# First batch, handover to the experts and final sums in another order, in a transformer layer kernel

## The chip, the cores and the metric

One core of a Trainium2 chip runs the whole program in one launch. The metric is the time of the slowest core on the device, in microseconds (us); there is one core here. Each kernel is timed over several runs, and one more execution is profiled.

## The reference

```python
x = x + attention(layernorm(x))     # x: 8 batches x 512 tokens x 256 channels
                                    # 16 heads of 16, rotary embedding, causal
x = x + moe(layernorm(x))           # 8 experts, top 2 of 8, capacity 153 per batch and expert
# moe: logits = h @ router_w + b ; p = softmax(top2(logits))
#      position of a token in its expert's buffer by a cumulative count over the batch
#      o = (silu((t @ w_c_fc + b1) * (t @ w_gate + b2))) @ w_c_proj + b3   (hidden 1024)
#      result = sum over the two experts of p * o[expert, position]
```

Layer norm has no weights. All is computed in float32. A product of float32 values is made of three TensorE products of high and low parts (`hi*hi + lo*hi + hi*lo`, `product3`, L79), so each operand is first split into a high part (rounded to fp32r) and a low part.

## The kernel before, in words

**Attention.** Batches run in a software pipeline of slots `(b, g, u)`: batch b, group g of four heads, slot u of eight. Each engine (SP for DMA issues, PE, ACT, DVE, POOL) runs its own hand-written list of what it does in a slot. The first batch has a prologue (`b = -1`): `load_x`, layer norm statistics on DVE (L729, L734), the inverse root on POOL (`rsqrt`, L947 to L955, three Newton steps, 14 instructions that each wait for the one before), `normalise` on DVE (L739), two sets of four transposes on PE ("X", L485), `xnT` split into high on ACT (L640) and low on DVE (L811), the q, k, v projections ("Q", "V"), the rotary embedding on DVE and POOL (L855, L856, L861, L973), and a high and low part `hilo` of the rotated q and k. SP stores `hilo[:, n]` to DRAM (`store_hilo`, L342; n = 0 is q and n = 1 is k of the first 128 channels, 512 KB each) and loads it back rearranged as `qst` and `kst` (`load_stack`, L355, 256 KB each, four per group of heads). PE's scores of a group (L450) wait for its four loads. Before the first projections, ACT copies the three weights to their high parts (L685) and DVE makes the low parts (L892) in the same queues.

**Handover.** The last batch's output row `x1` (L826), its second layer norm, router, slot numbers and scatter of token rows to `slot_tokens` are not done in the attention slots any more. `LATE_SLOTS` hangs them between the steps of the first expert: key -2 and -1 ahead of expert 0, key k behind step k (a step is one of 8 chunks of the hidden layer for one of three row blocks, so keys 0 to 7 are block 0, 8 to 15 block 1). In each slot stands an attention slot such as `(8, 3, 4)`, the last root on POOL, or `(9, 0, 1)`, the transposes of `hn`. The block 2 rows of expert 0 need the last scatter.

**Experts.** In each step PE makes the fc and gate products (`up`, L79), ACT adds the bias (L1458), DVE multiplies (`gated`, L1570), ACT applies silu (L1426), DVE casts to the high part `ah` (L1498), POOL makes the low part `al` (L1610). silu(k) waits for al(k-2). PE may be two steps ahead of `gated`. Behind step 2 PE projects the block before (`project`), and DVE adds the bias and writes `o_sb` (`tiles_out`, L1557), which SP stores to `slot_outputs`. POOL also splits the next expert's weights, one slice a step (L1644, L1649). The first expert's own weights are split by `split_first_hi` (L1098) and `split_first_lo` (L1103).

**Final sums.** In expert 7 POOL has no weights to split and gathers each token's two output rows from `slot_outputs` by indirect DMA (`gather`, L1675, four of 128 rows per batch and kind): the low ones (kind 0, expert numbers below) and the high ones (kind 1), each as soon as its stores have landed; the high ones of batches 5, 6 and 7 need the last tiles. `combine(b, k)` (L1542) on DVE adds four tiles of `share * gathered` to `y`, which starts as the residual `x1` that ACT's queue loads (`load_y`, L1438). ACT's queue also stores the results (`store_y`, L1443). `y` has four buffers for eight batches: a load for batch 4 to 7 waits for the store of batch b - 4. Where each stands is given by `LOAD_Y_AT` and `STORE_Y_AT` (block, step), `COMBINE_AT` (expert, block, tile) and `COMBINE_LAST`.

## Time and profile before

| What | us |
|---|---|
| Median of 3 runs (1255.8 to 1259.39) | 1258.95 |
| The profiled execution, its own time | 1255.67 |
| its span, first to last instruction | 1253.9 |
| busy: PE 1173.1 (94%), DVE 728.7, POOL 680.8, ACT 483.2 | |
| mean granted TensorE clock | 0.979 |
| issue of one stack load (L355) on SP's queue | 0.59 to 0.70 |
| a step of 384 columns on PE in the experts | 2.1 |
| a projection of three tiles on PE | 8.5 |
| POOL per step: split high 0.40, `al` 1.00, split low 0.74 | 2.15 |
| router: the two selections of one batch in the handover (L745 to L765), 563.50 to 567.3 | 3.8 |
| `split_first_lo` of one weight on DVE (L1103) | 2.28 |
| four tiles of a combine on DVE / one | 1.67 / 0.48 |
| `normalise`, four tiles, with POOL idle | 1.4 |
| wait of PE for `pv_sb` ahead of the first expert | 0.8 |
| end of the statistics of the last `x1` on DVE | 538.4 |

The span's busy shares are means over stages; what a wait costs is read in its stage. In the rows further down, times are in us from the span's start, durations in us, and in brackets stands how long the engine was idle before the group and what released it.

### The profile page before, as it was taken

How to read it: one execution, taken by the hardware profiler on the slowest of the kernel's cores; microseconds unless marked ns; L12 is line 12 of the kernel's file. 1: busy time of each engine (PE TensorE's matmuls, PEld its weight loads, DVE VectorE, ACT ScalarE, POOL GpSimd, SP SyncE). 2: the span in 40 equal slices, each digit the busy share in tenths (PEclk: the TensorE clock that was granted, in tenths of full speed). 3: DMA queues.
4: the chain of work that ended last, by engine and by line, in shares of the span. 5: the costliest groups of instructions: out<-in, count | busy, mean ns of one | idle time of the engine just before them, and what ended most of it. 6: DMA issues, size and time to landing. Idle time of an engine off the chain costs nothing.

```text
span 1253.9 us, 24021 instructions
## 1 busy us (share of the span) xinstructions
PE 1173.1 (94%) x8264; PEld 997.7 (80%) x8264; DVE 728.7 (58%) x1525; ACT 483.2 (39%) x988; POOL 680.8 (54%) x974
## 2 busy tenths in 40 slices
PE   4699999999999999878999999999999999999992
PEld 3466667676666666578999999999998999999992
DVE  5677788888888876656533333343333333434665
ACT  2146454545554545533332233233333222332320
POOL 4234342626363540677666556576665655667735
PEclk9699999999999999989999999999999999999996
DMA  5866845555555555333122122121211211304436
GB/s 138 222 238 193 243 120 151 139 149 151 140 147 144 143 141 148 118 135 107 60 69 64 64 73 98 41 96 59 69 59 62 73 64 65 113 26 132 147 122 209
DMA packets 83134, 148.24 MB, mean 118 GB/s; under 512 B 9647, under 2 KB 60728, under 8 KB 78910
## 3 DMA queue, kind: packets, MB, share of 16 engines
q1 hardware_dynamic: 65344, 111.37, 31.1%
q0 software_dynamic: 7936, 26.60, 6.3%
q10 hardware_dynamic: 9728, 8.67, 2.2%
q8 instruction: 69, 1.13, 0.4%
q14 instruction: 57, 0.47, 0.1%
HBM read 93.05 MB, written 53.61 MB: 117 GB/s over the span
## 4 chain that ended last, share of the span: by engine, by line
PE 49%; POOL 18%; issue 17%; DVE 9%; DMA 4%; ACT 2%; POOLq 0%; SPq 0%; DVEq 0%; ACTq 0%
PE ps L79 26%; POOL al L1610 8%; PE ps L450 5%; PE ps L479 4%; PE ps L468 3%; DVE mx L838 3%; PE ps L485 2%; PE ps L523 2%; POOL wp_lo L1649 2%; POOL wg_lo L1649 2%; PE ps L462 1%; DVE rope_s L855 1%; PE ps L441 1%; POOL wf L1649 1%; POOL wp_hi L1644 1%
## 5 line engine op out<-in xcount | busy, mean ns | idle before, releaser
L1610 POOL TENSOR_TENSOR al<-hid,ah 128x384 fp32r<-128x384 f32 (+1 forms) x168 | 179.3, 1067 | 209.0 <-DVE ah L1498 209.0
L1458 ACT ACTIVATE fc<-ps,b_fc 128x384 f32<-128x384 f32 (+1 forms) x192 | 115.4, 601 | 437.5 <-PE ps L79 436.4
L1570 DVE SCALAR_TENSOR_TENSOR gated<-ps,b_gate,fc 128x384 f32<-128x384 f32 (+1 forms) x192 | 123.2, 642 | 222.4 <-PE ps L79 201.8
L838 DVE TENSOR_REDUCE mx<-ps 128x2 f32<-128x256 f32 (+3 forms) x256 | 206.5, 819 | 34.2 <-PE ps L450 32.6
L450 PE MATMUL ps<-kst,qst 65*128 65x256 f32 (+2 forms) x512 | 149.1, 374 | 10.8 <-DMA kst<-qk_parts 10.8
L619 ACT ACTIVATE probs<-ps 128x512 f32<-128x512 f32 (+1 forms) x256 | 122.8, 542 | 54.4 <-PE ps L468 53.1
L1557 DVE TENSOR_TENSOR o_sb<-ps,b_proj 128x256 f32<-128x256 f32 x80 | 33.9, 424 | 153.9 <-PE ps L79 153.8
L1426 ACT ACTIVATE hid<-gated 128x384 f32<-128x384 f32 (+1 forms) x192 | 102.8, 536 | 25.8 <-POOL al L1610 14.4
L611 ACT ACTIVATE probs<-ps 128x256 f32<-128x256 f32 (+1 forms) x128 | 62.6, 490 | 128.2 <-PE ps L462 127.2
L79 PE MATMUL ps<-xh,wg_hi 128*128 128x384 f32 (+1 forms) x384 | 103.0, 349 | 3.7 <-DVE gated L1570 3.7
L79 PE MATMUL ps<-xl,wg_hi 128*128 128x384 f32 (+1 forms) x384 | 102.5, 348 | 0.0
L79 PE MATMUL ps<-xh,wg_lo 128*128 128x384 f32 (+1 forms) x384 | 102.3, 348 | 0.0
L1498 DVE CAST ah<-hid 128x384 fp32r<-128x384 f32 (+1 forms) x192 | 90.8, 473 | 9.5 <-ACT hid L1426 9.5
L479 PE MATMUL ps<-probs,v_sb 128*17 128x512 f32 (+3 forms) x1024 | 93.8, 438 | 0.0
L79 PE MATMUL ps<-xh,wf 128*128 128x384 f32 (+1 forms) x384 | 89.3, 354 | 1.6 <-DVE xl L1409 0.9
L450 PEld LDWEIGHTS ps<-kst,qst 65*128 65x128 f32 x512 | 80.2, 198 | 11.1 <-DMA kst<-qk_parts 11.0
L79 PE MATMUL ps<-wp_hi,ah 128*128 128x256 f32 (+1 forms) x632 | 87.6, 281 | 1.4 <-DVE posm L778 0.9
L79 PE MATMUL ps<-wp_lo,ah 128*128 128x256 f32 (+1 forms) x632 | 87.5, 281 | 0.0
L79 PE MATMUL ps<-wp_hi,al 128*128 128x256 f32 (+1 forms) x632 | 87.3, 280 | 0.0
L973 POOL TENSOR_TENSOR rope_c<-qk_b,rope_table 128x512 f32<-128x512 f32 x32 | 43.7, 1365 | 75.4 <-ACT qk_b L647 75.3
L79 PEld LDWEIGHTS ps<-wp_hi,ah 128*128 128x128 f32 (+1 forms) x632 | 80.8, 183 | 2.6 <-issue 1.2
L79 PEld LDWEIGHTS ps<-wp_lo,ah 128*128 128x128 f32 (+1 forms) x632 | 79.8, 184 | 0.0
(194 smaller groups left out, 2461.9 us busy)
## 6 DMA issues: line engine op xcount, KB each, us to landing
qk_parts<-hilo SPq DMA_DIRECT2D x32, 512.0 KB, 3.7
qst<-qk_parts SPq DMA_DIRECT2D x64, 256.0 KB, 5.0
kst<-qk_parts SPq DMA_DIRECT2D x64, 256.0 KB, 5.6
slot_tokens<-zeros POOLq DMA_DIRECT2D x12, 816.0 KB, 5.9
rows<-slot_tokens SPq DMA_DIRECT2D x24, 384.0 KB, 3.6
slot_outputs<-o_sb SPq DMA_DIRECT2D x72, 128.0 KB, 1.7
raw<-in_wf SPq DMA_DIRECT2D x8, 1024.0 KB, 6.8
raw<-in_wg SPq DMA_DIRECT2D x8, 1024.0 KB, 6.8
```

Source lines behind the costliest of these rows:

```text
L79: last = nc.tensor.matmul(out, w, x, start=(i == 0), stop=(i == len(terms) - 1))
L450: last = mm(bank, qst[0:MROW, g, h, bass.ts(i, P)], kst[0:MROW, g, h, 0:width], start=False, stop=True, skip_group_check=True)
L479: last = mm(pvb[32 * h:32 * h + DH + 1, P * j:T], v_sb[:, bt % 2, j, GH * g + h, :], probs[:, j % 2, h, P * j:T], start=(j == 0), stop=(j ...
L611: A(probs[:, j % 2, 2 * pr:2 * pr + 2, P * j:T], in_pairs(banks2(u)[0])[:, :, P * j - q0:T - q0], ACT.Exp, scale=float(DH) ** -0.5).then_i ...
L619: A(probs[:, j % 2, 2 * pr + hh, P * j:T], ps[:, banks2(u)[hh], P * j - q0:T - q0], ACT.Exp, scale=float(DH) ** -0.5).then_inc(exp_done, 1)
L838: V.reduce_max(mx[:, g % 2, 2 * pr:2 * pr + 2, i], both[:, :, 0:P * (i + 1)], AXX)\
L1426: A(hid[:, hc % 2, 0:width], gated[:, hc % 2, 0:width], ACT.Silu).then_inc(hid_done, 1)
L1458: A(fc[:, hc % 2, 0:width], ps[:, FC + hc % 2, 0:width], ACT.Identity, bias=b_fc[:, e, hc:hc + 1]).then_inc(fc_out, 1)
L1498: V.tensor_copy(ah[:, (8 * n + hc) % RING, 0:width], hid[:, hc % 2, 0:width]).then_inc(ah_done, 1)
L1570: V.scalar_tensor_tensor(gated[:, hc % 2, 0:width], ps[:, GATE + hc % 2, 0:width], b_gate[:, e, hc:hc + 1], fc[:, hc % 2, 0:width], ALU.ad ...
L1610: G.tensor_tensor(al[:, at, 0:width], hid[:, hc % 2, 0:width], ah[:, at, 0:width].bitcast(F32), ALU.subtract).then_inc(al_done, 1)
L1649: ins = G.tensor_tensor(w_lo[1 - par][n][:, cols], src, w_hi[1 - par][n][:, cols].bitcast(F32), ALU.subtract)
```

## The change

- Batch 0's inverse root moves from POOL to DVE (`root`, 11 chained instructions), and so does the root of the last batch's second layer norm; the other roots stay on POOL. The memsets of `base` and `v_sb` go to the front of DVE's list. On ACT and DVE the evictions of the first transposes come ahead of the weights' high and low parts. SP loads the rotary table ahead of `wvT`.
- The first two stores of `hilo` are cut in halves of 64 channels, each with a semaphore; the q loads of the first stack wait only for q's half, the k loads for k's.
- `LATE_SLOTS`: the root in key 1 of DVE, `hn` in key 2 in place of 3; transposes, router and scatters one key earlier; `split_first_lo(2)` in step 4 in place of 2 and with a wait for itself ahead of the count.
- `y` gets eight buffers (four of them over gathered rows that are already summed), residual loads start at step 0 of expert 7, all low sums are made before the last steps, batches 5 to 7 are combined tile by tile as each gather lands (`FINE = 5`), and their results go out in halves.

```diff
@@ -340,6 +341,21 @@
         sp.dma_start(dst.rearrange("h p t -> p h t"), hilo[:, n].bitcast(F32)).then_inc(st_hilo[n // 2], 16)
+    def store_first(n, part):
+        wait(sp, hilo_done, n + 1)
+        side = slice(GH * DH * part, GH * DH * (part + 1))
+        dst = rt["qk"][0, n, :, side, :].rearrange("h p t -> p h t")
+        sp.dma_start(dst, hilo[side, n].bitcast(F32)).then_inc(st_hilo[0] if part else st_first[n], 16)
+    def load_first_stack(n):
+        sp.wait_ge(st_first[n], 16)
+        for i in range(2):
+            q = rt["qk"][0, 0, :, 0:GH * DH, :].rearrange("c (d h) t -> d c (h t)", h=GH)
+            k = rt["qk"][0, 1, i, 0:GH * DH, :].rearrange("(d c h) t -> d c (h t)", h=GH, c=1)\
+                .to_broadcast([DH, 2, GH * T])
+            rows = (qst, kst)[n][2 * DH * i:2 * DH * (i + 1), 0].rearrange("r h t -> r (h t)").bitcast(F32)
+            sp.dma_start(rows, (q, k)[n]).then_inc(ld_stack[0], 16)
@@ -391,14 +407,19 @@
     for i, (w_sb, name) in enumerate(((raw_q, "wqT"), (raw_k, "wkT"), (raw_v, "wvT"))):
+        if i == 2:
+            sp.dma_start(rope_table, d["consts"][:, 0:2 * T]).then_inc(ld_w, 16)
...
-    sp.dma_start(rope_table, d["consts"][:, 0:2 * T]).then_inc(ld_w, 16)
...
-    for n in range(4):
+    store_first(0, 0)
+    store_first(1, 0)
+    store_first(0, 1)
+    load_first_stack(0)
+    load_first_stack(1)
+    store_first(1, 1)
+    for n in range(2, 4):
...
-        if n == 1:
-            load_stack(0, 0)
@@ -680,11 +701,11 @@
     A(lgT[:, 0:1], wr[:, 0, E:E + 1], ACT.Exp)
+    body_slot(-1, 0, 7)
+    body_slot(-1, 1, 0)
...
-    body_slot(-1, 0, 7)
-    body_slot(-1, 1, 0)
@@ -738,6 +759,19 @@
                                   ALU.subtract, ALU.mult)
+        ins.then_inc(done, 1)
+    def root(chain, mv, rs, done):
+        v, y, a = rs[:, 0, :], rs[:, 1, :], rs[:, 2, :]
+        chain(V.tensor_scalar(v, mv[:, :, 1], EPS, None, ALU.add))
+        chain(V.tensor_scalar(y.bitcast(I32), v.bitcast(I32), -0.5, RSQRT_MAGIC, ALU.mult, ALU.add))
+        for it in range(3):
+            chain(V.tensor_tensor(a, y, y, ALU.mult))
+            chain(V.scalar_tensor_tensor(a, a, -0.5, v, ALU.mult, ALU.mult))
+            ins = V.scalar_tensor_tensor(y, a, 1.5, y, ALU.add, ALU.mult)
+            if it < 2:
+                chain(ins)
@@ -863,6 +897,10 @@
             layer_stats(chain, x1, stats2, mv2, mv2_done)
+        if (g, u) == (3, 4) and isinstance(b, int) and b == BATCH:
+            dve.wait_ge(mv2_done, BATCH)
+            dve.wait_ge(rs2_done, BATCH - 1)
+            root(chain, mv2, rs2, rs2_done)
@@ -883,7 +921,11 @@
     V.memset(wr[:], 0.0).then_inc(wr_set, 1)
+    chain(V.memset(base[:], float(E * EROWS)))
+    chain(V.memset(v_sb[:], 1.0))
...
+    dve.wait_ge(mv1_done, 1)
+    root(chain, mv1, rs1, rs1_done)
@@ -897,19 +939,17 @@
-    split_lo(0)
-    split_lo(1)
-    body_slot(chain, -1, 0, 7)
-    body_slot(chain, -1, 1, 0)
-    split_lo(2)
...
-    chain(V.memset(base[:], float(E * EROWS)))
-    chain(V.memset(v_sb[:], 1.0))
+    body_slot(chain, -1, 0, 7)
+    body_slot(chain, -1, 1, 0)
+    split_lo(0)
+    split_lo(1)
+    split_lo(2)
@@ -1026,7 +1066,7 @@
     G.memset(zeros[:], 0.0).then_inc(z_ready, 1)
-    for g, u in ((0, 1), (1, 2), (1, 5), (1, 7), (2, 2)):
+    for g, u in ((1, 2), (1, 5), (1, 7), (2, 2)):
@@ -1099,8 +1140,10 @@
 eng.wait_ge(w_half, j + 1)
+ops.tensor_tensor(w0[1][j], raw[:, j % 2, :], w0[0][j].bitcast(F32), ALU.subtract).then_inc(w_lo_done[j], 1)
+eng.wait_ge(w_lo_done[j], 1)
...
-ops.tensor_tensor(w0[1][j], raw[:, j % 2, :], w0[0][j].bitcast(F32), ALU.subtract).then_inc(w_ready, 1)
+eng.sem_inc(w_ready, 1)
@@ -1111,12 +1154,12 @@
 "pe": {-2: ((8, 2, 3),), -1: ((8, 2, 5), (8, 2, 6)), 0: ((8, 3, 1), (8, 3, 2)),
-   5: ((9, 0, 1), (9, 0, 2)), 6: ((9, 0, 4),), 7: ((9, 0, 5),), 9: ((9, 1, 5),)},
-"act": {-2: ((8, 2, 2),), -1: ((8, 2, 6), (8, 2, 7)), 5: ((9, 0, 2), (9, 0, 3)), 6: ((9, 0, 5),), 8: ((9, 1, 4),)},
-"dve": {-2: ((8, 2, 4),), 0: ((8, 3, 2), (8, 3, 3)), 1: ((8, 2, 6),), 3: ((8, 3, 7),),
-    7: ((9, 0, 6), (9, 1, 1), (9, 1, 2)), 9: ((9, 1, 6), (9, 2, 1)), 10: ((9, 2, 6),)},
-"pool": {-1: ((8, 2, 3), (8, 2, 4), (8, 2, 6)), 0: ((8, 3, 4),),
-     9: ((9, 2, 1), (9, 2, 3), (9, 2, 4), (9, 2, 6))},
+   4: ((9, 0, 1), (9, 0, 2)), 5: ((9, 0, 4),), 6: ((9, 0, 5),), 8: ((9, 1, 5),)},
+"act": {-2: ((8, 2, 2),), -1: ((8, 2, 6), (8, 2, 7)), 4: ((9, 0, 2), (9, 0, 3)), 5: ((9, 0, 5),), 7: ((9, 1, 4),)},
+"dve": {-2: ((8, 2, 4),), 0: ((8, 3, 2), (8, 3, 3)), 1: ((8, 3, 4),), 2: ((8, 3, 7),), 3: ((8, 2, 6),),
+    6: ((9, 0, 6), (9, 1, 1), (9, 1, 2)), 8: ((9, 1, 6), (9, 2, 1)), 10: ((9, 2, 6),)},
+"pool": {-1: ((8, 2, 3), (8, 2, 4), (8, 2, 6)),
+     8: ((9, 2, 1), (9, 2, 3), (9, 2, 4), (9, 2, 6))},
@@ -1182,29 +1225,37 @@
 got_late = [half for w_ in (w_hi, w_lo) for half in in_batches(w_[0][2][:].bitcast(F32))]
-y = [half for i in range(2) for half in in_batches(raw[:, i, :])]
+spent = Region(nc, rt["early"])
+spent.skip(4 * 2 * 2 * HID)
+y_rows = [raw[:, 0, :], raw[:, 1, :], spent.take("y_spent0", [P, 2 * HID])]
+spent.skip(2 * 4 * 2 * HID)
+y_rows.append(spent.take("y_spent1", [P, 2 * HID]))
+y = [half for tile in y_rows for half in in_batches(tile)]
+FINE = 5
...
-got_low, got_high = ([sem(f"got_{kind}{b}") for b in range(BATCH)] for kind in ("low", "high"))
-ld_y = [sem(f"ld_y{i}") for i in range(len(y))]
-st_y = [sem(f"st_y{i}") for i in range(len(y))]
-summed, low_sum = sem("summed"), sem("low_sum")
+got_low, got_high = ([sem(f"got_{kind}{b}") for b in range(n)] for kind, n in (("low", BATCH), ("high", FINE)))
+ld_y = [sem(f"ld_y{i}") for i in range(BATCH // 2)]
+st_y = sem("st_y")
+summed, low_sum, half_sum = sem("summed"), sem("low_sum"), sem("half_sum")
+got_row = [[sem(f"got_row{b}_{i}") for i in range(TT)] for b in range(FINE, BATCH)]
...
-LOAD_Y_AT = ((0, 3), (0, 4), (0, 5), (0, 6))
-STORE_Y_AT = ((2, 6), (2, 7))
+LOAD_Y_AT = ((0, 0), (0, 1), (0, 2), (0, 3), (0, 4), (0, 5), (0, 7), (1, 1))
+STORE_Y_AT = ((2, 4), (2, 5))
+COMBINE_IN = {(0, 5): (2, 0), (0, 7): (3, 0), (1, 5): (7, 0), (2, 5): (2, 1)}
...
-    (LAST, 0, 1): ((2, 0),), (LAST, 0, 2): ((3, 0),),
+    (LAST, 0, 0): ((4, 0),), (LAST, 0, 1): ((5, 0),), (LAST, 0, 2): ((6, 0),),
...
-    (LAST, 2, 0): ((2, 1),), (LAST, 2, 1): ((3, 1),), (LAST, 2, 2): ((4, 0),), (LAST, 2, 3): ((5, 0),),
+    (LAST, 2, 0): ((3, 1),), (LAST, 2, 1): ((4, 1),),
...
-COMBINE_LAST = ((4, 1), (6, 0), (5, 1), (7, 0), (6, 1), (7, 1))
+COMBINE_LAST = ((5, 1), (6, 1), (7, 1))
@@ -1388,9 +1438,9 @@
-    late_slots("pe", 0, -2)
...
+    late_slots("pe", 0, -2)
@@ -1433,14 +1483,19 @@
             act.wait_ge(rt["st_x1"], 16 * BATCH)
-        if b >= len(y):
-            act.wait_ge(st_y[b % len(y)], 16)
-        act.dma_start(y[b % len(y)], batch_rows(rt["x1"], b)).then_inc(ld_y[b % len(y)], 16)
+        if b >= BATCH // 2:
+            act.wait_ge(low_sum, b - BATCH // 2 + 1)
+        act.dma_start(y[b], batch_rows(rt["x1"], b)).then_inc(ld_y[b % (BATCH // 2)], 16)
...
-        act.wait_ge(summed, b + 1)
-        act.dma_start(batch_rows(d["out"], b), y[b % len(y)]).then_inc(st_y[b % len(y)], 16)
+        if b < FINE:
+            act.wait_ge(summed, b + 1)
+            act.dma_start(batch_rows(d["out"], b), y[b]).then_inc(st_y, 16)
+            return
+        for i in range(2):
+            act.wait_ge(half_sum, 2 * (b - FINE) + i + 1)
+            act.dma_start(batch_rows(d["out"], b)[:, 2 * i:2 * i + 2], y[b][:, 2 * i:2 * i + 2]).then_inc(st_y, 16)
@@ -1471,13 +1526,7 @@
-    load_y(4)
-    load_y(5)
-    store_y(2)
-    load_y(6)
-    store_y(3)
-    load_y(7)
-    for b in range(len(y), BATCH):
+    for b in range(2, BATCH):
@@ -1530,18 +1579,25 @@
+        fine = k == 1 and b >= FINE
...
-            dve.wait_ge(ld_y[b % len(y)], 16 * (b // len(y) + 1))
+            dve.wait_ge(ld_y[b % (BATCH // 2)], 16 * (b // (BATCH // 2) + 1))
...
-            dve.wait_ge(got_high[b], 16 * TT)
+            if not fine:
+                dve.wait_ge(got_high[b], 16 * TT)
...
-            ins = V.scalar_tensor_tensor(y[b % len(y)][:, t, :], src[:, t, :], share[:, k, col:col + 1],
-                                         y[b % len(y)][:, t, :], ALU.mult, ALU.add)
-        ins.then_inc((low_sum, summed)[k], 1)
+            if fine:
+                dve.wait_ge(got_row[b - FINE][t], 16)
+            ins = V.scalar_tensor_tensor(y[b][:, t, :], src[:, t, :], share[:, k, col:col + 1],
+                                         y[b][:, t, :], ALU.mult, ALU.add)
+            if fine and t % 2 == 1:
+                ins.then_inc(half_sum, 1)
+        if not fine:
+            ins.then_inc((low_sum, summed)[k], 1)
@@ -1575,11 +1631,13 @@
                     sort_entries(hc)
-                if isinstance(e, int) and (e, n, hc) == (0, 0, 2):
+                if isinstance(e, int) and (e, n, hc) == (0, 0, 4):
...
+                if isinstance(e, int) and e == LAST and (n, hc) in COMBINE_IN:
+                    combine(*COMBINE_IN[n, hc])
@@ -1675,7 +1733,8 @@
                 in_offset=bass.IndirectOffsetOnAxis(ap=row_of[:, k, col:col + 1], axis=0),
-                bounds_check=there_now - 1, oob_is_err=False).then_inc((got_low, got_high)[k][b], 16)
+                bounds_check=there_now - 1, oob_is_err=False)\
+                .then_inc(got_row[b - FINE][t] if k == 1 and b >= FINE else (got_low, got_high)[k][b], 16)
```

## Rows read from the trace of the kernel before

**Rows 1.** Windows: length, busy PE, PEld, DVE, ACT, POOL, PEclk, DMA, GB/s.
```profile
39.00:60.00 21.00, 17.80 (x68) 12.26 (x68) 14.70 (x30) 2.83 (x5) 5.34 (x17) 0.58 0.96 261
545.00:560.00 15.00, 7.32 (x48) 6.64 (x46) 6.40 (x11) 5.35 (x11) 13.69 (x30) 0.77 0.19 69
610.00:1150.00 540.00, 537.37 (x3494) 522.63 (x3493) 203.73 (x417) 173.39 (x344) 338.25 (x458) 1.00 0.21 71
```

**Rows 2.** Timeline, first batch: start, us, engine, line, operation, idle before it.
```profile
10.88 1.38 DVE L739 TENSOR_SCALAR xn<-x_in,mv,rs 128x256 f32<-128x256 f32 x4 [4.01 <-POOL rs L955]
...
12.77 0.69 DVE L892 TENSOR_TENSOR wq_lo<-raw_q,wq_hi 128x512 fp32r<-128x512 f32 x1 [0.51 <-ACT wq_hi L685]
...
14.86 1.06 ACT L640 ACTIVATE xnT_hi<-ps 128x512 fp32r<-128x512 f32 x2
15.47 1.29 DVE L811 TENSOR_TENSOR xnT_lo<-ps,xnT_hi 128x512 fp32r<-128x512 f32 x2 [1.04 <-ACT xnT_hi L640]
...
16.91 1.19 PE L79 MATMUL ps<-xnT_hi,wq_hi 128*128 128x512 f32 x2 [2.57 <-DVE xnT_lo L811]
...
18.59 1.87 DVE L912 MEMSET v_sb<- 128x2176 f32 x1 [0.54 <-DVE base L911]
...
39.13 0.79 PE L450 MATMUL ps<-kst,qst 65*128 65x256 f32 x2 [10.75 <-DMA kst<-qk_parts]
```

**Rows 3.** Timeline of PE, expert 0: transposes of hn and last rows.
```profile
554.65 1.94 PE L485 MATMUL ps<-consts_sb,hn 128*128 128x128 f32 x8 [7.68 <-DVE hn L739]
...
589.35 0.98 PE L1332 MATMUL ps<-consts_sb,rows 128*128 128x128 f32 x8 [1.34 <-DMA rows<-slot_tokens]
```

**Rows 4.** Timeline of POOL, last root, first al after it, last scatters.
```profile
544.93 0.22 POOL L947 TENSOR_SCALAR rs<-mv 128x4 f32<-128x4 f32 x1
...
549.11 0.99 POOL L1610 TENSOR_TENSOR al<-hid,ah 128x384 fp32r<-128x384 f32 x1
...
573.71 1.13 POOL L1005 DMA_INDIRECT slot_tokens<-hn,put_at  x1 [1.44 <-DVE put_at L790]
```

**Rows 5.** Timeline of ACT, expert 0.
```profile
550.19 0.52 ACT L1426 ACTIVATE hid<-gated 128x384 f32<-128x384 f32 x1 [8.19 <-POOL al L1610]
```

**Rows 6.** Timeline of PE, expert 7, after that combine.
```profile
1156.29 0.62 PE L79 MATMUL ps<-xh,wg_hi 128*128 128x384 f32 x2 [2.27 <-DVE gated L1570]
```

**Rows 7.** Timeline of DVE, expert 7: combine of batch 1.
```profile
1153.70 1.67 DVE L1542 SCALAR_TENSOR_TENSOR raw<-wf_hi,share,raw 128x256 f32<-128x256 f32 x4 [7.98 <-DMA raw<-x_rows]
```

**Rows 8.** Timeline of POOL, gathers in expert 7 and after it.
```profile
1154.00 1.06 POOL L1675 DMA_INDIRECT wf_lo<-slot_outputs,row_of  x1 [0.31 <-issue]
...
1227.18 0.99 POOL L1675 DMA_INDIRECT wp_hi<-slot_outputs,row_of  x1 [8.84 <-issue]
...
1231.08 3.17 POOL L1675 DMA_INDIRECT wp_hi<-slot_outputs,row_of  x1 [0.30 <-issue]
...
1241.30 2.86 POOL L1675 DMA_INDIRECT wp_lo<-slot_outputs,row_of  x1 [0.30 <-issue]
...
1245.77 0.99 POOL L1675 DMA_INDIRECT wp_lo<-slot_outputs,row_of  x1 [0.30 <-issue]
```

**Rows 9.** Timeline of DVE, the last combine.
```profile
1248.64 1.67 DVE L1542 SCALAR_TENSOR_TENSOR raw<-wp_lo,share,raw 128x256 f32<-128x256 f32 x4 [5.36 <-DMA wp_lo<-slot_outputs,row_of]
```

**Rows 10.** Timeline of DVE, small steps of one chain (four of them).
```profile
490.78 0.16 DVE L770 TENSOR_SCALAR dlt<-ex 128x4 f32<-128x4 f32 x1
...
491.39 0.17 DVE L773 TENSOR_TENSOR prob_all<-ex,dlt 128x4 f32<-128x4 f32 x1
```

**Rows 11.** Chain of waits, first 45 us: start, us, what.
```profile
28.46 2.75 DMA qk_parts<-hilo
...
33.19 5.89 DMA kst<-qk_parts
```

**Rows 12.** DMA issues, whole span: KB each, median us to landing.
```profile
slot_outputs<-o_sb SPq DMA_DIRECT2D x72, 128.0 KB, 1.7
...
out_rows<-raw ACTq DMA_DIRECT2D x8, 512.0 KB, 3.3
```

11 lines of the change are left out of this document (6 added, 5 removed).

## Prediction

> **What bounds the kernel now.** Durations without a group stand in the table of the profile above. I read the windows first. From 610 to 1150 us TensorE is busy 537.4 of 540 us at the full clock [rows 1], and the change edits nothing there. Time can only come from the three places that it edits: the first batch, the handover from attention to experts, and the end. For those I read the chain of waits and then each engine's timeline.
>
> *First batch.* TensorE's first scores start at 39.13, after 10.75 us of waiting for the key stack [rows 2]. Before that the chain is serial: statistics, the root on POOL (VectorE idle for 4.01), xn, transposes, the two splits of xnT, projections, rotation, the store, the load of the stack.
>
> *Handover.* TensorE stands 7.68 us before it transposes the last batch's hn and 1.34 before the last token rows [rows 3]. The first is a knot of queues: POOL does its root of 14 steps from 544.93, ahead of the first `al`, at 549.11 [rows 4]; ScalarE's next silu waits 8.19 for that `al` [rows 5]; VectorE's cast waits for the silu, and hn stands behind the cast.
>
> *End.* Expert 7 loses 2.27 on TensorE [rows 6], because VectorE waited 7.98 for a residual load that ScalarE's queue issued only after the projection [rows 7]. After TensorE is done, 12 gathers leave POOL from 1227.18 on, 1.3 apart (0.99 and a gap of 0.30), except two that take 3.17 and 2.86. The last is issued at 1245.77 [rows 8], its combine starts at 1248.64 [rows 9], and one 512 KB store follows.
>
> **The change, part by part.**
>
> *Root of batch 0 on VectorE.* POOL's 14 steps go and VectorE gets 11. Four chained steps of VectorE on small tiles lie 0.20 apart: 490.78 to 491.39 is three pitches [rows 10]. So 11 x 0.21 = 2.3 in place of 4.0, a gain of 1.7. xn starts at 9.2 rather than 10.88 and ends at 10.6. The memset of v_sb (1.87) [rows 2] and the tiny one of base move in front; x takes longer than that to land, so they cost nothing. Had x landed at once, they would cost 1.9.
>
> *Transposes before weight splits.* The 8 transposes take 1.94 on a cold clock, as the same eight do later [rows 3], so they end at 12.6. The last xnT_hi (1.06 for two) ends at 13.1 and its xnT_lo (1.29 for two) at 13.8. wq is now copied behind xnT_hi and split behind xnT_lo: 0.69 for the split [rows 2], ending at 14.5. VectorE's five bf16 casts move ahead of this, while it waits for the transposes. Q0 starts at 14.7 instead of 16.91: 2.2 gained, the root included. The table of rope passes raw_v in SP's queue; wv is needed last of the three, so I cost this at nothing. All that follows up to the second `hilo` keeps its order, so it moves by 2.2.
>
> *Half stores.* Now: the store after the second `hilo` takes 2.75, then four loads of some 0.65 each to issue, of which the last goes out at 33.19 and lands 5.89 after that [rows 11]. From 28.46 that is 4.73 to the last issue. New: two half stores (0.55 each to issue), two q loads (0.65 each) while the k half store lands, one k load: the last issue is 3 x 0.65 + 2 x 0.55 = 3.1 after `hilo`, and 3.3 with the wait for the k half, 1.4 gained. A half store is 256 KB; between 1.7 for 128 KB and 3.3 for 512 KB [rows 12] it takes about 2.2, so it is down before the k loads. But the loads fill the DMA engines (0.96 busy from 39 to 60) [rows 1], and the remaining halves and later stores now share them, so I take 1.2. Bounds: 0 if the engines' throughput sets the landing, 1.7 if the half store lands at once. A rule speaks against this part: the Trainium skill ("DMA: Bandwidth & Descriptors", the section "Anatomy of one DMA") gives a DMA some 2 us however small, plus its bytes at 436 GB/s, and the section "Bandwidth" advises large ones. By an estimate from that page a half store still takes 2.6 and this part brings 0.8, not 1.2; the 1.7 for 128 KB in the rows is under its fixed part, so I stay with the rows.
>
> First batch: 2.2 + 1.2 = 3.4, between 2.2 and 3.9. The later stacks land before their turn, so I let all of it through.
>
> *Handover* (on the time axis of before, without the shift of the first batch). The root goes to VectorE at step 1, hn to step 2, split_first_lo(2) from 2 to 4, and all router pieces one step earlier. POOL's first `al` moves up by 3.9. Statistics end at 538.4, the root takes 2.3 behind one gated product: 542.2. Then the next product and cast, and hn of 1.4: 544.6. TensorE reaches the H pieces at 544.6: the 7.68 is gone. What is late next? ScalarE's copies of hT stand behind silu(3), which waits for the second `al`, at 548.4: hT is out at 550.2, and TensorE, done with its next step at 547.8, waits 2.4. From there POOL's pace is 2.15 per step, about TensorE's own 2.1. VectorE adds the split (2.28) and the router's two selections (about 4.0), which hold `onehot` to 559; scatters start at 565.1 instead of 573.71 [rows 4], and the last rows are transposed at 581 rather than 589.35 [rows 3]. Gain 8.0. Bounds: 3.9, the root alone; 10.2, if the route does not fall behind the split. The sem_inc behind the split costs 0.1 on VectorE. Moving turn 0 before the A piece fills a wait of 0.8 for pv_sb and costs nothing.
>
> *Low sums earlier.* ScalarE now issues its residual loads from step 0 on, so the 2.27 goes. The price: the first load waits for the last weight split of POOL, and ScalarE's first step is some 2.5 late; TensorE runs two steps ahead on banks, so I charge 0.3, which the projection's slack gives back. VectorE gets low combines (1.67 each) at steps 5, 7 and 13 and waits at two of them for gathers, up to 2.6 behind; TensorE's slack is 2.1 per step, so I charge nothing. If that cover were gone, each late combine would cost up to 1.7.
>
> *End.* Before, at the two long gathers VectorE ran 8 and 12 combine rows in a stretch while 512 KB residual loads and stores filled the DMA engines. Both causes leave: low combines and loads are done by then. So 3.17 + 2.86 - 2 x 0.99 = 4.05 comes out of the chain. The last combine is one row of 0.48 and not four (1.67): 1.2. The last store is 256 KB: 3.3 - 2.2 = 1.1. With the 2.27: 8.6. Bounds: 4.6 if the long gathers stay, 9.0 if the last landing (2.8) is also quicker, with less in flight.
>
> Sum: 3.4 + 8.0 + 8.6 = 20.0. The profiled execution took 1255.67 for a span of 1253.9; less 20.0 that is 1235.7. It lies 3.3 below the median of the three runs, which would give 1239.0. I say 1237.
>
> **Rivals.**
>
> *The gathers stay long.* If the stall is POOL's own ring that fills when transfers queue, 12 gathers 1.3 apart can still fill it. The gain is then 16, so 1241. For it: both long ones came after several in flight. Against: the other 62 gathers took 1.32 at most, many of them with three in flight too.
>
> *Each row's combine holds the next gather.* A gather beside a combine took 1.06 [rows 8], against 0.99, so the hold is small by this row. If each of the 11 combine rows that now fall between gathers held one up by its whole 0.48, the end would get 5.3 back and the gain would be 14.7: 1242. That is how the Trainium skill ("SBUF — State Buffer", the section "SBUF: two separate sides") describes VectorE with two SBUF inputs, or in a two-port mode, against GpSimd: the other blocks for the whole instruction.
>
> *The handover gives the root only.* If `al` and hid pace it and the router falls behind split_first_lo, 3.9 comes and not 8: gain 16, 1241.
>
> *Slower.* From 545 to 560 the granted clock was 0.77 in the mean, and from 39 to 60, with small waits, 0.58 (near 1.2 GHz) [rows 1]. If the new wait of 2.4 at the L piece leaves it at 1.2 GHz, TensorE's work from there to the last rows, 10 steps of 2.1 and a projection of 8.5, takes twice its 29.5: 1237 + 29.5 = 1266. It decides from 22 us of doubled work on, 44 us at the low clock. For it: one wait of 7.68 was enough to pull the mean to 0.77. Against it: from 39 to 60 the clock did come back, with waits beside it.
>
> *It does nothing:* each path is hidden behind another, 1259. Against it: TensorE or the last gathers stand alone on the chain in every one of the three.
>
> **How the numbers follow.** Forecast (all three parts) 0.63; long gathers 0.13; combine holds gathers 0.10; root only 0.10; low clock 0.02; nothing 0.02. The bounds of the parts sum to gains of 10.7 and 23.1 together; from the median the first is 1248, from the profiled execution the second is 1232. Range 1231 to 1247. A measurement of this kernel tells 0.3% (3.8 us) from no change; all cases but the last two are faster by more: faster 0.95, same 0.03, slower 0.02.
>
> **What would show it.** xn at 9.2, Q0 at 14.7, the first scores near 35.7; hn before 545 + the shift of the first batch, with no wait of 7.68 at its transposes but one of 2 to 3 at L; the last token rows near 578; no wait of VectorE for residual loads in expert 7; the 12 last gathers 1.3 apart with none over 1.5, and 2.8 from the last one to its one combine row. It is wrong if the key stack lands after 37, if a new wait over 4 stands in the handover, if gathers beside single combine rows take 1.4, or if the clock stays at half after 545.

## The result, and the profile after

The changed kernel took 1244.0 us in the median (1242.8 to 1245.3, 4 runs) against 1258.5 for the kernel before (1255.8 to 1259.4, 4 runs): ratio 0.9888, 95% interval 0.9868 to 0.9909. That is 14.5 us less where 20 were forecast; 1244 lies inside the range. The profiled execution has a span of 1240.8 against 1253.9. The sections below show that some 3.4 of these microseconds come from something the forecast did not contain, and that two of its three sums were too large.

**First batch**, timeline of VectorE and TensorE after the change, for [rows 2]:

```profile
7.12 0.17 DVE L767 TENSOR_SCALAR rs<-mv 128x4 f32<-128x4 f32 x1
...
9.10 0.16 DVE L772 SCALAR_TENSOR_TENSOR rs<-rs 128x4 f32<-128x4 f32 x1
9.30 1.38 DVE L760 TENSOR_SCALAR xn<-x_in,mv,rs 128x256 f32<-128x256 f32 x4
...
14.03 0.68 DVE L934 TENSOR_TENSOR wq_lo<-raw_q,wq_hi 128x512 fp32r<-128x512 f32 x1
...
14.77 1.22 PE L79 MATMUL ps<-xnT_hi,wq_hi 128*128 128x512 f32 x2 [2.01 <-DVE wq_lo L934]
...
35.64 0.80 PE L471 MATMUL ps<-kst,qst 65*128 65x256 f32 x2 [9.44 <-DMA kst<-qk_parts]
```

The root's 11 steps start at 7.12 and end at 9.26; xn starts at 9.30, Q0 at 14.77, the scores at 35.64. The forecast said 9.2, 14.7 and 35.7. The half stores themselves were slower than it said (2.2); the DMA issues of this profile give their size and the median from issue to landing:

```profile
qk_parts<-hilo SPq DMA_DIRECT2D x4, 256.0 KB, 3.3
```

**Handover**, waits of TensorE from 545 to 600 us (us in total, times, longest), then its timeline and POOL's first `al`, for [rows 3, 4]:

```profile
PE ps L79 <- DVE xl L1459: 3.0, 2, 2.7
PE ps L567 <- DVE onehot_bf L798: 2.3, 1, 2.3
PE ps L555 <- ACT hT L679: 1.8, 1, 1.8
...
544.47 1.00 POOL L1668 TENSOR_TENSOR al<-hid,ah 128x384 fp32r<-128x384 f32 x1
...
582.01 0.96 PE L1382 MATMUL ps<-consts_sb,rows 128*128 128x128 f32 x8
...
587.87 0.68 PE L79 MATMUL ps<-xh,wf_hi 128*128 128x456 f32 x2 [2.75 <-DVE xl L1459]
```

The wait of 7.68 for hn is gone, one of 1.80 stands at the L piece, and the last rows are transposed at 582.01 instead of 589.35, without a wait. But there is a new one, 2.75 for `xl`, ahead of block 2. That block starts at 587.87; before it started at 592.96. So 7.3 us of lead at the rows are 5.1 at the block behind them. (The forecast had the rows near 578 with the first batch's lead; the third batch's xn stands at 99.5 in both profiles, so that lead does not show here. In a second profile of the changed kernel it does, and the rows are at 579.8.)

**Expert loop.** Nothing in it was changed, and yet TensorE gained 1.7 us there twice. Timeline of VectorE at the two returns of the loop over experts, in the kernel before, and at the first of them after:

```profile
796.12 0.62 DVE L1570 SCALAR_TENSOR_TENSOR gated<-ps,b_gate,fc 128x384 f32<-128x384 f32 x1 [4.66 <-issue]
...
966.26 0.62 DVE L1570 SCALAR_TENSOR_TENSOR gated<-ps,b_gate,fc 128x384 f32<-128x384 f32 x1 [4.67 <-issue]
```
```profile
788.19 0.62 DVE L1626 SCALAR_TENSOR_TENSOR gated<-ps,b_gate,fc 128x384 f32<-128x384 f32 x1 [1.77 <-ACT fc L1513]
```

Before, VectorE stood 4.7 us at each return (the jump back to the first instruction of the loop) with nothing that the profile shows to wait for ("issue"). After, it waits 1.77 for ScalarE, as a step normally does.

**End.** Waits of TensorE from 600 us on, the 12 last gathers (first and last), the last combine row and the stores, for [rows 6 to 9, 12]:

```profile
PE ps L79 <- DVE xl L1459: 2.2, 2, 1.3
...
1219.24 1.00 POOL L1733 DMA_INDIRECT wp_hi<-slot_outputs,row_of  x1 [9.64 <-issue]
1220.54 1.00 POOL L1733 DMA_INDIRECT wp_hi<-slot_outputs,row_of  x1 [0.30 <-issue]
...
1233.57 1.00 POOL L1733 DMA_INDIRECT wp_lo<-slot_outputs,row_of  x1 [0.30 <-issue]
...
1236.50 0.48 DVE L1595 SCALAR_TENSOR_TENSOR y_spent<-wp_lo,share,y_spent 128x256 f32<-128x256 f32 x1 [0.33 <-DMA wp_lo<-slot_outputs,row_of]
...
out_rows<-y_spent ACTq DMA_DIRECT2D x6, 256.0 KB, 2.8
slot_outputs<-o_sb SPq DMA_DIRECT2D x6, 128.0 KB, 1.7
```

None of these 12 gathers took over 1.0; they need 14.3 us from the first issue to the last, against 18.6. VectorE waits for no residual load. In the place of TensorE's 2.27 [rows 6] there are 1.28 and 0.88 for `xl`. The last combine row starts 2.93 behind the last gather's issue (forecast 2.8), but 3.82 us pass between its end and the end of the span, no less than before (3.59).

### How the profiles are compared

Profiles of the same code differ in one stretch by more than the changes that are to be seen. So each profile is cut at the same instructions: the first scores, `xn` of the third batch, POOL's first `al` of expert 0, block 2 of expert 0, one expert's first tile to the same tile an expert later (`o_sb` of experts 2 to 3 and 4 to 5, the loop's returns), the first tile of expert 6, the first of the last 12 gathers, the last gather, the end. Durations in us:

| Kernel | scores at | scores to xn 3 | xn 3 to block 2 | return 1, 2 | expert 6 to gathers | 12 gathers | last gather to end |
|---|---|---|---|---|---|---|---|
| before | 39.13 | 60.5 | 493.4 | 86.0, 86.1 | 142.6 | 18.6 | 8.1 |
| after | 35.64 | 63.9 | 488.3 | 84.3, 84.3 | 143.1 | 14.3 | 7.2 |
| `first_only` | 36.07 | 61.7 | 493.4 | 84.3, 84.2 | 142.9 | 16.8 | 8.8 |
| `handover_only` | 39.90 | 65.5 | 489.0 | 84.7, 84.4 | 142.6 | 16.7 | 8.7 |
| `end_only` | 40.46 | 65.0 | 492.9 | 85.8, 86.0 | 143.0 | 14.3 | 7.2 |
| `before_pad25` | 38.99 | 63.3 | 493.4 | 84.2, 84.3 | 143.1 | 17.3 | 8.6 |
| `root_only` | 39.33 | 62.0 | 492.0 | 84.2, 84.2 | 143.2 | 17.1 | 8.8 |
| `first_whole_stores` | 37.40 | 61.8 | 493.3 | 84.3, 84.2 | 142.9 | 17.0 | 8.8 |
| `after_again` | 35.58 | 61.9 | 488.0 | 84.5, 84.2 | 142.6 | 14.3 | 7.2 |
| `three_more` | 35.52 | 63.8 | 486.9 | 84.2, 84.2 | 141.0 | 14.4 | 7.2 |

### The profile page after: what moved, and what is told of

It reads as the page before. It is cut to its first block, busy times and chain, and to the rows that moved or that the text cites. A ratio compares the mean times of both kernels' runs of the same rounds, so it can differ in the third digit from the quotient of the medians.

```text
span 1240.8 us, 24020 instructions
## 1 busy us (share of the span) xinstructions
PE 1172.2 (94%) x8264; PEld 997.3 (80%) x8264; DVE 738.1 (59%) x1547; ACT 483.1 (39%) x988; POOL 675.5 (54%) x946
## 4 chain that ended last, share of the span: by engine, by line
POOL 26%; issue 20%; PE 6%; DVE 2%; DMA 1%; POOLq 1%; ACT 0%; DVEq 0%; ACTq 0%
POOL al L1668 11%; PE ps L79 6%; POOL wp_lo L1707 3%; POOL wg_lo L1707 3%; POOL wp_hi L1702 1%; POOL wg_hi L1702 1%; POOL wf L1707 1%; POOL wf_lo L1707 1%; POOL wf_hi L1702 1%; POOL wf L1702 1%; POOL slot_tokens L1045 0%; POOL wp_hi L1733 0%; DMA wf_lo<-slot_outputs,row_of 0%; POOL wp_lo L1733 0%; DVE ah L1547 0%
## 5 line engine op out<-in xcount | busy, mean ns | idle before, releaser
L1013 POOL TENSOR_TENSOR rope_c<-qk_b,rope_table 128x512 f32<-128x512 f32 x32 | 43.4, 1357 | 80.8 <-ACT qk_b L668 80.7
```

## The experiments

### One part of the change at a time

The change falls into three parts that build alone. From here on all ratios are to the kernel before, run in the same group on the same chip.

`first_only`: the hunks of the first batch, without those of `LATE_SLOTS`, `split_first_lo` and the final sums.

> The kernel before with the first batch's part of the change alone (root on VectorE, memsets in front, transposes ahead of the weight splits, half stores); handover and end as before. Theory 1, from the two traces: the first scores start 3.5 us earlier, but all of it is lost again between 53 and 70 us (VectorE's rotary products beside POOL's, then TensorE at half its clock for longer), so the third batch's xn starts at 99.5 as before and the time falls by 0.1 us. The two stalls of VectorE of 4.7 us at the expert loop's return, near 796 and 966, stay or go with the place of the code: if they go too, another 3.4 us. Theory 2, the forecast's: 3.4 us of the lead reach the end, 1255.1 in place of 1258.5.

Measured: 1251.2 against 1259.1, ratio 0.9943 (0.9928 to 0.9959). Theory 1 had been read from two profiles and fell: 7.9 us less, not 0.1 or 3.5. Both stalls at the loop's return are gone (3.5), and the rest, some 4, is the lead. The column "scores to xn 3" says why the two profiles misled: kernels whose code there is identical took 60.5, 65.5, 65.0, 63.3 and 62.0 us over it. The first profile of before is the shortest of them. One thing that differs is the course of TensorE's clock. Windows of the kernel before and of `end_only`, the same code up to 1130 us (columns as in [rows 1]):

```profile
60.00:70.00 10.00, 8.18 (x40) 6.01 (x41) 9.80 (x16) 3.54 (x6) 7.61 (x8) 0.84 0.42 168
70.00:80.00 10.00, 9.95 (x81) 6.59 (x80) 7.47 (x11) 4.02 (x10) 3.50 (x4) 0.99 0.48 172
```
```profile
60.00:70.00 10.00, 6.33 (x34) 4.21 (x33) 9.97 (x13) 2.46 (x4) 5.49 (x6) 0.92 0.34 137
70.00:80.00 10.00, 10.00 (x57) 7.46 (x56) 5.91 (x9) 4.25 (x9) 5.08 (x6) 0.74 0.33 126
```

In one execution the clock is full from 70 us on (0.99), in the other it is 0.74 there in the mean, and TensorE gets 57 matmuls done in place of 81. But the clock alone does not explain it. In `handover_only`, the slowest, the clock leaves 0.50 within 2 us of the place where it does in the kernel before (windows of 2 us: 0.84 in 56 to 58 there, 0.93 in 58 to 60 here), and both keep the same pace up to 17 us behind the first scores. Then comes a product of VectorE with two inputs in SBUF that starts within 0.13 us of one of POOL's. The kernel before, then `handover_only`:

```profile
60.05 1.85 POOL L973 TENSOR_TENSOR rope_c<-qk_b,rope_table 128x512 f32<-128x512 f32 x1 [2.24 <-ACT qk_b L647]
60.06 0.68 DVE L861 TENSOR_TENSOR rope_s<-rope_c,rope_s 128x512 f32<-128x512 f32 x1
```
```profile
61.06 1.28 POOL L990 TENSOR_TENSOR rope_c<-qk_b,rope_table 128x512 f32<-128x512 f32 x1 [2.49 <-ACT qk_b L647]
61.19 1.70 DVE L874 TENSOR_TENSOR rope_s<-rope_c,rope_s 128x512 f32<-128x512 f32 x1
```

Once POOL is held (1.85 in place of 1.28), once VectorE (1.70 in place of 0.68). In `handover_only` VectorE's next such product, beside POOL's, takes 1.76 in place of 0.96 as well, and at 34 us behind the first scores it is 2.2 us late. In the seven profiles of all in which this product takes 0.68, the stretch is 60.5 to 62.0 us, and 63.6 in one; in the seven in which it takes 1.65 to 1.75, it is 63.3 to 65.5. The other 2.8 us of `handover_only` were not traced step by step. The means over the five profiles with the old prologue and over seven with the new one are 63.3 and 62.8, so within some 1 us the lead is kept.

`handover_only`: `LATE_SLOTS`, the last root, `split_first_lo`, turn 0 first.

> The kernel before with the handover's part alone (last root on VectorE, hn, router and scatters one step earlier, the third low split two steps later). Theory 1: the last token rows are transposed 7.3 us earlier, but block 2 of expert 0 starts only 5.1 earlier, since POOL's pace of 2.15 us per step and its eight scatters set it, with a wait of TensorE of 2 to 3 us for xl; the time falls by 5.1 us, or by 8.5 if VectorE's two stalls at the loop's return go as well. Theory 2, the forecast's: 8.0 us.

Measured: 1250.6, ratio 0.9931 (0.9913 to 0.9950), 8.5 less. "xn 3 to block 2" is 489.0 against 493.4, the stalls are gone: 4.4 and 3.0. Theory 1 holds for the size; the new wait for `xl` ahead of block 2 is 1.64 here, under the 2 to 3 it said.

`end_only`: the eight buffers of `y`, early loads and low sums, rows, halves.

> The kernel before with the final sums' part alone. VectorE's code up to the end of the loop over experts has the same length as before. Theory 1: VectorE's two stalls of 4.7 us at the loop's return stay, and the end gives 4.7 us: 4.2 from the gathers being even, 0.5 to 1.5 from the rest, the wait of 2.27 being mostly replaced by new ones for xl. Theory 2, the forecast's: 8.6 us.

Measured: 1253.5, ratio 0.9955 (0.9939 to 0.9972), 5.6 less. Both stalls stay (85.8 and 86.0). Before the last gathers nothing is gained (143.0 against a mean of 142.9 in the six kernels with the old end), the 12 gathers give 2.9 against the mean of those six (17.2), the tail 1.4 (8.6). That is 4.3, inside the interval of the time (3.5 to 7.7 us), where the forecast's 8.6 is not: theory 1 holds. The profile of before had an unlucky second long gather, which none of the other five has.

### Where VectorE's code lies

`before_pad25` adds nothing but this, at the front of VectorE's list:

```diff
+for _ in range(25):
+    dve.sem_inc(padding, 1)
```

> The kernel before with 25 increments of an unused semaphore at the front of VectorE's list, where it waits for x. Nothing else. They move VectorE's code for the loop over experts to where it stands after the change: the loop begins at its instruction 1207 in place of 1182. Theory 1 (the two stalls of VectorE of 4.7 us at the loop's return hang on where the code lies): both go, TensorE gets 1.7 us back at each, the time falls by 3.4 us. Theory 2 (something else in the change took them away, or they come and go by chance): both stay, no change.

Measured: 1254.5 against 1259.1, ratio 0.9968 (0.9958 to 0.9979). Both stalls are gone, at each return TensorE is 1.8 us quicker. Theory 1 holds: 25 instructions that do nothing make this kernel 4 us faster. The next one moves the same loop, in the changed kernel, to 256 instructions behind its old place:

> The changed kernel with increments of an unused semaphore among VectorE's instructions in the attention batches, until its code of the expert loop begins at instruction 1438, which is 256 behind where it began before the change (1182) and 231 behind where it begins after it (1207). Theory 1 (code comes in pieces of 256 instructions and what counts is where the loop lies in them): the two stalls of 4.7 us are back, TensorE waits some 1.7 at each, and the time is 3.4 us above the changed kernel's, 1247.5. Theory 2 (it is something else in those 25 increments): no stall, and the time of the changed kernel or up to 2 us more for the increments themselves.

(241 increments make the code 231 instructions longer.) Timeline of VectorE at both returns:

```profile
808.04 0.62 DVE L1630 SCALAR_TENSOR_TENSOR gated<-ps,b_gate,fc 128x384 f32<-128x384 f32 x1 [4.38 <-issue]
...
978.03 0.62 DVE L1630 SCALAR_TENSOR_TENSOR gated<-ps,b_gate,fc 128x384 f32<-128x384 f32 x1 [4.51 <-PE ps L79]
```

The stalls are back, 4.38 and 4.51 (the second is put down to TensorE, but its length and place are the same), and the two stages take 85.8 and 85.9. It is this timeline that decides; the time cannot, since the changed kernel itself was not run in this group. The loop is 354 instructions long. It stalls where it begins at 1182 or 1438, and not at 1194, 1195 or 1207. The Trainium skill ("Runtime: NRT & Kernel Launch", the section "Instruction fetch mechanics") says that an engine but TensorE holds two blocks of 256 instructions, and that a jump back to a block that is no longer held waits for a fetch. A period of 256, and a loop of 354 that fits into two blocks from some places and needs three from others, agree with it. At which instruction a block begins no run shows directly. An estimate from the 256 of this section of the Trainium skill and from the runs: a loop of 354 needs three blocks when it begins at 1182 and two when it begins at 1194 to 1207 only if a block begins between instruction 1183 and 1194.

The group of four kernels that this one ran in (with `after_put_off`, `after_whole_sums` and `after_warm`) took some 4% longer throughout (before 1309.3, this one 1303.9, ratio 0.9964, 0.9939 to 0.9988). Some 15 to 18 us of that are waits of TensorE behind the loop that no other group shows; another 15 to 19 us lie between xn 3 and block 2, which takes 504 to 507 us in this group. Ratios within the group stand, times are not to be set beside the others. Waits of TensorE in `after_whole_sums` from 1150 to 1190 us:

```profile
PE ps L79 <- issue: 17.5, 15, 3.0
```

### Half stores

`first_whole_stores` is `first_only` with the old `store_hilo` and `load_stack` for the first group.

> The first batch's part without the half stores. With them the first scores started at 35.3 to 36.1 us in five profiles, without any of the part at 39.0 to 40.5 in four. By the forecast's terms the root, the memsets and the order of the splits give 2.2 and the half stores 1.2: here the scores start at 36.7 to 37.3. If the half stores give nothing, 35.5; if they give all that the engines' queues allow, 37.5 or later.

Measured: 1253.4, ratio 0.9968 (0.9951 to 0.9985); the scores start at 37.40. Means: old prologue 39.6 (five profiles), this one 37.4, with half stores 35.6 (seven). So 2.2 and 1.8, where 2.2 and 1.2 were forecast. But 37.4 is one profile. In it and in `first_only`, `handover_only` and `end_only` a product of VectorE ahead of the second `hilo` (it starts at 20.26 to 22.56 us) takes 1.67 to 1.76 beside one of POOL's and not 0.69 as in the others, so the means mix two courses. Counted from the end of the second `hilo`, behind that product, the scores start 10.5 to 11.4 us later in the six profiles with whole stores (mean 10.9; 10.5 in this kernel) and 9.2 to 9.4 in the seven with half stores (mean 9.3). So the half stores give 1.2 by this kernel and 1.5 by the means: the forecast's term was right, and its upper bound of 1.7 was not passed.

### What a moved root alone brings

```diff
-0: ((8, 3, 2), (8, 3, 3)), 1: ((8, 2, 6),), 3: ((8, 3, 7),)
+0: ((8, 3, 2), (8, 3, 3)), 1: ((8, 3, 4), (8, 2, 6)), 3: ((8, 3, 7),)
```

> The kernel before with the last root alone on VectorE, in step 1 of expert 0; hn, router, scatters and the third low split where they were before. Theory 1 (POOL's work, from its first al on, sets block 2 of expert 0, so that only what leaves POOL counts): from the third batch's xn to block 2 it takes 488.5 us as with the whole handover (488.3 and 489.0), not 493.4 as before; the two stalls at the loop's return are gone as well, since the loop begins at instruction 1194: 8.5 us in all. Theory 2, the forecast's: the root gives 3.9, and the steps that moved give 4.1 more, so 489.5 here against 485.4 with all of it.

Measured: 1252.0, ratio 0.9943 (0.9927 to 0.9960); "xn 3 to block 2" is 492.0. Both theories fell: the root alone gives 1.3 (the mean of the five profiles with the old handover is 493.3), though 14 steps left POOL. Timelines of VectorE and POOL in `root_only`:

```profile
545.23 2.49 DVE L1120 TENSOR_TENSOR wp_lo<-raw,wp_hi 128x2048 fp32r<-128x2048 f32 x1
...
545.66 2.64 POOL L1666 TENSOR_TENSOR wf<-raw,wf 128x256 fp32r<-128x256 f32 x1
...
548.64 1.01 POOL L1627 TENSOR_TENSOR al<-hid,ah 128x384 fp32r<-128x384 f32 x1
```

and in the kernel before:

```profile
541.49 2.28 DVE L1103 TENSOR_TENSOR wp_lo<-raw,wp_hi 128x2048 fp32r<-128x2048 f32 x1
...
542.73 1.31 POOL L1644 TENSOR_SCALAR wf<-raw 128x256 fp32r<-128x256 f32 x1 [1.67 <-DMA raw<-in_wf]
544.13 0.73 POOL L1649 TENSOR_TENSOR wf<-raw,wf 128x256 fp32r<-128x256 f32 x1
```

The third low split (two inputs in SBUF, 2.3 to 2.5 us) used to run mostly while POOL waited for its weights, and only stretched POOL's high split at its end (1.31, where it otherwise takes 0.40). With the root ahead of it, it falls on POOL's own low split, which takes 2.64 in place of 0.73, and the first `al` comes 1.9 later than it could. The Trainium skill ("SBUF — State Buffer", the section "SBUF: two separate sides") describes this: of a VectorE instruction with two SBUF inputs and a GpSimd one, whichever starts first keeps the shared port for its whole instruction. The trace agrees: here VectorE started 0.43 earlier. So putting `split_first_lo(2)` two steps later, which the forecast took for a mere delay of the router, accounts for 1.9 of the 3.5 us between the root alone and the whole handover; the rest lies with the steps that also moved. No run moved the split by itself.

### Who sets block 2

Code in short form; the whole edit puts POOL's slices of four steps off.

```diff
+PUT_OFF = (1, 2, 3, 4)      # steps of block 1, expert 0
...
+if put_off: pool.sem_inc(w_split, 1)
+else: G.tensor_scalar(w_hi[1 - par][n][:, cols], src, ...)
...
+if (e, n, hc) == (0, 2, 3): # four slices in one: high, then low
```

> The changed kernel with POOL's weight slices of steps 1 to 4 of block 1 in expert 0 (4 times 1.14 us of splits) made in one piece at step 3 of block 2, beside TensorE's projection. Theory 1 (POOL's total work from the scatters on sets when block 2 of expert 0 starts): the wait of 2.75 us for xl ahead of block 2 goes nearly to nothing, and 2 to 2.7 us are kept to the end. Theory 2 (the wait comes from xh and xl standing behind hid and ah in their queues, and these are as late without the splits): the wait stays above 2 us and nothing is gained.

Measured: 1297.5, ratio 0.9917 (0.9885 to 0.9949), the lowest ratio of its group, with intervals that overlap. From the first `al` to block 2 it takes 46.3 us against 49.6, 49.9 and 50.8 in the three others of the group, whose code there is the changed kernel's. TensorE does not wait ahead of block 2, but in this slower group it does not in the three others either, so that says nothing for either theory; `three_more` below is the test, in a group with the usual times. The big piece ran only behind the next `al`, at 621 to 625 us, and 1.8 us were lost in the following block. `three_more` puts it ahead of the projection and adds two edits:

```diff
-COMBINE_IN = {(0, 5): (2, 0), (0, 7): (3, 0), (1, 5): (7, 0), (2, 5): (2, 1)}
+COMBINE_IN = {(0, 6): (2, 0), (0, 7): (3, 0), (1, 6): (7, 0), (2, 5): (2, 1)}
...
 split_in(dve, e2, n2, side(par, n + 1), c, False)
+if ... (n, hc) in COMBINE_IN: combine(*COMBINE_IN[n, hc])   # was ahead of it
...
 store_y(2)
+act.wait_ge(st_o[tile % OB], ...)      # tile = TB[2] + 1, of expert 7
 for b in range(3, BATCH): store_y(b)
```

> The changed kernel with three more edits. POOL's slices of steps 1 to 4 of block 1, expert 0, in one piece behind step 2 of block 2, ahead of its idle stretch beside the projection (behind it, in the kernel tried before, they held an al and gave 2.1 of 3.5 us back): theory 1 says 3.3 us from POOL's first al to block 2 are gained and kept. In expert 7 the combines of batches 2 and 7 stand one step later and behind the split of x: the waits for xl of 1.3 and 0.9 us go, 1 to 2 us. The results of batches 3 and 4 are stored only once the tile that the gathers of batch 5 need has landed: these start 1.1 us earlier. In all 5 to 6 us under the changed kernel. Theory 2: POOL's gathers are paced by themselves and what TensorE gains in expert 7 is lost at them, as it was with the change itself; then 4 us.

> The changed kernel once more, for a second profile and as the measure for the other kernels of this call. The stretch from the first scores to the third batch's xn took between 60.5 and 65.5 us in profiles of identical code; everything behind it should stand as in the first profile: 445 us from that xn to POOL's first al, 43.4 from there to block 2 of expert 0, 84.3 over each return of the expert loop, 14.3 for the last 12 gathers, 7.2 from the last one's issue to the end.

Measured: `after_again` 1242.2 against 1257.3, ratio 0.9873 (0.9854 to 0.9891); `three_more` 1237.5, ratio 0.9835 (0.9821 to 0.9850). No run of the one (1239.9 to 1244.0) is as quick as any of the other (1236.3 to 1239.7). So this version beats both kernels, by 4.7 us the changed one. Waits of TensorE from 600 us on and start of the last gathers in `three_more`:

```profile
PE ps L79 <- ACT fc L1515: 0.4, 2, 0.3
PE ps L79 <- DVE gated L1631: 0.3, 1, 0.3
...
PE ps L79 <- DVE xl L1461: 0.2, 1, 0.2
...
1215.14 1.00 POOL L1750 DMA_INDIRECT wp_hi<-slot_outputs,row_of  x1 [8.46 <-issue]
```

From xn 3 to the end it takes 1137.4 us, against 1141.3 and 1141.9 in the two profiles of the changed kernel. From the first `al` to block 2 it takes 41.6 us against 43.4 in both profiles of the changed kernel, and the wait of 2.75 is gone: what POOL has to do sets block 2. But "xn 3 to block 2" fell by 1.1 to 1.4 only, less than theory 1 said: TensorE then has its own waits for hT and onehot (2.1 and 2.3) further up. In expert 7 the 2.2 for `xl` have shrunk to 0.2, and the gathers kept that, against theory 2. And the gathers of batch 5 start 2.98 us behind the tile they need, as in every kernel with the old end (2.98 to 3.07), where after the change it was 4.18 (4.13 in `after_again`). Windows of the changed kernel in that stretch:

```profile
1213.00:1214.00 1.00, 1.00 (x11) 1.00 (x10) 1.00 (x4) 0.00 (x0) 0.00 (x0) 1.00 0.00 0
1214.00:1215.00 1.00, 1.00 (x11) 1.00 (x10) 1.00 (x3) 0.00 (x0) 0.00 (x0) 1.00 0.94 317
1215.00:1216.00 1.00, 1.00 (x11) 1.00 (x10) 0.45 (x2) 0.00 (x0) 0.00 (x0) 1.00 1.02 325
1216.00:1217.00 1.00, 1.00 (x11) 1.00 (x10) 0.00 (x0) 0.00 (x0) 0.00 (x0) 1.00 1.01 349
1217.00:1218.00 1.00, 1.00 (x11) 1.00 (x10) 0.11 (x1) 0.00 (x0) 0.00 (x0) 1.00 0.93 319
```

From 1214 to 1218 the DMA engines are full (0.93 to 1.02) with results of 512 KB, and the tile's 128 KB, issued at 1215.5, go through between them. With the change these stores fall on this tile. It hangs on the moment: in the slower group two kernels with the same early stores start these gathers 3.0 and 3.1 us behind the tile, the two others 4.2 and 5.0.

### The last sums

`after_whole_sums` sets `FINE = 8`: batches 5 to 7 are summed whole and stored whole, the rest is as changed.

> The changed kernel with the last three batches summed whole again: four tiles of combine once all four gathers have landed, one store of 512 KB each. Residual loads and low sums stay early. Theory 1: the gathers stay at 1.3 us each, since what stretched two of them were residual loads, stores and long runs of combines together, and these are still gone; from the last gather's issue to the end of the span it takes 8.1 us as before the change, in place of 7.2. Theory 2 (runs of combines hold gathers): a gather beside a whole combine takes 1.6 to 3 us again, the 12 gathers take 16 to 18 us in place of 14.3. The forecast's terms for this part were 1.2 for the combine and 1.1 for the store.

Measured: ratio 0.9932 (0.9906 to 0.9957). Timeline of POOL and VectorE:

```profile
1279.83 0.99 POOL L1733 DMA_INDIRECT wp_lo<-slot_outputs,row_of  x1 [0.30 <-issue]
1281.13 1.10 POOL L1733 DMA_INDIRECT wp_lo<-slot_outputs,row_of  x1 [0.30 <-issue]
...
1287.75 1.00 POOL L1733 DMA_INDIRECT wp_lo<-slot_outputs,row_of  x1 [0.30 <-issue]
...
1280.09 1.67 DVE L1595 SCALAR_TENSOR_TENSOR y_spent<-wp_hi,share,y_spent 128x256 f32<-128x256 f32 x4 [3.79 <-DMA wp_hi<-slot_outputs,row_of]
...
1291.74 1.67 DVE L1595 SCALAR_TENSOR_TENSOR y_spent<-wp_lo,share,y_spent 128x256 f32<-128x256 f32 x4 [4.05 <-DMA wp_lo<-slot_outputs,row_of]
```

The gathers stay even: 14.4 us for the 12, and the one beside a whole combine took 1.10. So it is not the rows that made them even, and theory 2 falls for a combine of four rows; what is left is that loads, low sums and long runs of combines are over by then. Which of these stretched a gather to 3.1 was not tried. The traces point at the runs: in all six profiles with the old end the gather of 3.13 to 3.19 began inside a run of eight combine rows on VectorE and ended 0.9 behind it. But a run of 12 rows stretched one gather to 2.86 in the kernel before and three to 1.22 to 1.28 in `before_pad25`, so the run alone does not fix the length. From the last gather's issue to the end it took 9.15 against 7.2 in the three others of the group: 2.0 in this pair, of which 1.2 is the shorter combine and 1.1 the landing (3.99 from issue to combine here, 2.93 in the changed kernel), and nothing the halved store (3.49 from combine to end here, 3.82 there). The landing of 3.99 is the longest of all: in the six profiles with the old end, also with whole sums, it is 2.87 to 3.61 (mean 3.4), in the seven with the new end and rows 2.90 to 3.25 (mean 3.0). So the 1.4 that the tail gained is 1.2 for the combine, 0.4 for the landing and -0.2 for the store.

### Keeping the clock up

```diff
+for _ in range(36):   # between the first mask and the wait for the key stack
+    mm(ps[:, 1, :], ident_bf[:], causal_bf[:] broadcast to 512 columns, start=True, stop=True)
```

> The changed kernel with 36 extra products of 512 bf16 columns on TensorE, into a bank nobody reads before it is written again, between its first mask and its wait for the key stack. They fill most of the 9.4 us that it waits there. In every profile so far the clock is full up to that wait and at 1.2 GHz from its end on, until some time between 56 and 78 us, and in that stretch identical code took up to 6 us more or less. Theory 1 (the wait costs the clock): the 36 products take 8 us, the granted clock is 1.0 from 36 us on, the third batch's xn starts 4 to 8 us earlier than 99.5, and the time falls to some 1238. Theory 2 (VectorE sets the pace there and the clock does not matter): xn at the same place, 1244. Theory 3 (the clock falls anyway, since TensorE has little to do until 60 us): half clock from about 40 on, gain under 1 us; if the clock is at half already during the products, they take 15 us and delay the scores by 7.

Measured: ratio 0.9950 (0.9925 to 0.9976), no better than the others of its group; xn 3 at 100.7 against 96.4, 99.1 and 99.1 in the three others. Timeline of TensorE:

```profile
25.84 7.93 PE L592 MATMUL ps<-causal_bf,ident_bf 128*128 128x512 bf16 x36
36.11 0.51 PE L471 MATMUL ps<-kst,qst 65*128 65x256 f32 x2 [2.34 <-DMA kst<-qk_parts]
...
37.19 0.78 PE L471 MATMUL ps<-kst,qst 65*128 65x256 f32 x2
```

The 36 products took 7.9 us, so at the full clock, and the first scores ran at it (0.51 for two; 0.80 in the changed kernel). One microsecond later the same instruction takes 0.78. Theory 3 has the outcome: the clock falls anyway. Its reason (TensorE has little to do) is not shown, since 2.34 us of waiting for the key stack stayed between the products and the scores.

## Why the forecast was right, and where it was wrong

**First batch, 3.4.** Right, with each milestone within 0.1, and in both its terms: 2.2 for root and order, 1.2 to 1.5 for the half stores. (The raw means of the scores differ by 4.0; some 0.2 of that is the slower course of VectorE's product, which two of five profiles with the old prologue have and one of seven with the new one.) Two readings inside the second term were off all the same: a half store took 3.3 in the median to land and not 2.2, and the full DMA engines were read from a window behind the first scores (39 to 60 us). The lower figure that the forecast drew from the Trainium skill ("DMA: Bandwidth & Descriptors", the section "Anatomy of one DMA"), 0.8, is further off; that section is about DMAs that GpSimd issues, and these leave SP's queue.

**Handover, 8.0.** The mechanism was right up to the last rows (7.3 us earlier, the wait at L, POOL's pace behind it), and 4.8 arrive (488.4 against 493.3 in the means). The step that failed is "the last rows are transposed at 581 rather than 589.35: gain 8.0": rows transposed are not rows usable. `xh` stands behind `hid` in ScalarE's queue, `hid` waits for `al`, and POOL, which the forecast itself had pacing, has its eight scatters (10 us) and four more steps to do first. POOL's first `al` came 4.6 earlier, and that is what is left at block 2. The rival "the root only" gave 3.9 and was near the size, but not for its reason: the root alone brings 1.3. The wait at L, forecast as 2 to 3, was 1.8; the one of 2.75 for `xl` was not forecast.

**End, 8.6.** 4.3 arrive. Term by term: the 2.27 in expert 7 was gained as 1.2 (to the tile that the last gathers need) and lost again at that tile's store (1.2 more until the gathers start; the forecast charged nothing for the new combines and did not look at what the earlier stores meet); the two long gathers gave 2.9, not 4.05, since the second of them belonged to that one execution; the last combine gave its 1.2, and the landing 0.4; the store's 1.1 did not come: 256 KB take 2.8 to land and not 2.2. That does not explain all of it; that the two halves leave one queue one after the other may be the rest, which no run shows. The rivals that gathers stay long, or are held by each row, are excluded: 0.99 to 1.00 beside eleven single rows, each with two inputs in SBUF. The slower rival did not come either: the granted clock from 540 to 592 us is 1.00 (0.93 before).

**Not in the forecast: 3.4** at the loop's returns. "From 610 to 1150 the change edits nothing" was true of the work and not of the code's place.

**Sum:** 3.7 + 4.8 + 4.3 + 3.4 = 16.2, against 14.1 (11.5 to 16.6) and 16.0 (13.7 to 18.4) in two measurements. The forecast of 1237 was also anchored half at the profiled execution, which had the luckiest stretch of all between scores and xn 3 (60.5; the mean is 63.3). Set against the median, its own sum gives 1239. Without the code's place the kernel would stand near 1247.4, 8 us above that and just outside the range of 1231 to 1247 (the bounds of its parts, set against the median, would have given 1248). So the first part was right, the two others were right in kind and too large, and that the total came out inside the range is in part luck.

## What to carry to other kernels

Follow a moved step to the instruction that uses its result, through the queue that it stands in, and ask which engine's whole work lies between. When an edit adds or takes instructions ahead of a loop, look at the loop's return in the profile ("issue" waits there); a few idle instructions can be worth more than the edit. And take a second profile of the unchanged kernel before you believe a difference in a stretch where the clock changes, or where instructions of VectorE and POOL start within some 0.1 us of each other.

## What was not expected of the hardware

- A loop of 354 instructions on VectorE stalls by 4.4 to 4.7 us at each return, or not at all, by where it lies; moved on by 256 it stalled again.
- A product of VectorE with two inputs in SBUF stretched a POOL instruction that started 0.43 later from 0.73 to 2.64. Where two such instructions start within 0.13 us of each other, now one is held and now the other (0.68 or 1.70 on VectorE), and the stretch with them took 60.5 to 65.5 us in executions of the same code.
- The granted clock stood at 0.50 from the first scores on and came back between 53 and 61 us; in 12 of 14 profiles it fell again, for 3 to 7 us, between 62 and 76 us. 8 us of added products ahead, with 2.3 us of waiting behind them, did not keep it up.
- In one group TensorE waited 17.5 us for "issue" within 40 us behind the loop, at some 1 us each, in one profile and much the same in the three others, and all kernels were 4% slower. What that was stays open.
